# The first stage of a two-layer transformer tower: head sums turned by DVE and a DMA round trip, and the next batch's steps in other bursts

## The reference, cut to what matters

```
emb = x @ W + pe                                  # 1024 x 128, kept in H
n0  = layernorm(emb)                              # without gain and bias
Q, K, V = n0 @ Wq.T + bq, n0 @ Wk.T + bk, n0 @ Wv.T + bv
Q, K, V = (t.reshape(B * 8, 1024, 16) for t in (Q, K, V))   # a plain reshape: a "head" is 128 tokens x 8 pieces of 16 columns
context = softmax(Q @ K.T / 4) @ V                # reshaped back to 1024 x 128
r   = context @ Wo.T + bo + n0
H   = emb + layernorm(r) * gamma + beta           # the residual stream
mean1, rstd1 = moments of H; score1 = (layernorm of H) . attn_w   # for the next stage
```

## Time and profile before

| | us |
|---|---|
| median of 3 runs (1563.72 to 1567.42) | 1564.57 |
| the profiled execution | 1566.77 |
| its span in the trace | 1564.5 |
| first exponential of the first stage | 61.7 |
| the last copy of psO in the first stage | 669.5 |
| PE, DVE, ACT busy over the whole span | 1250.5, 989.6, 1012.1 |

### The profile page before, as it was taken

One profiled execution on the slowest core, in us unless ns is written; L12 is line 12 of the kernel. 1 busy time (PEld: TensorE's weight loads), 2 busy tenths in 40 slices (PEclk: granted clock), 3 DMA queues, 4 the chain that ended last, 5 costly groups with the idle time before them and its releaser, 6 DMA issues. The chain is left out here.

```text
span 1564.5 us, 30966 instructions
## 1 busy us (share of the span) xinstructions
PE 1250.5 (80%) x9689; PEld 826.3 (53%) x9689; DVE 989.6 (63%) x2772; ACT 1012.1 (65%) x1358; POOL 520.9 (33%) x456
## 2 busy tenths in 40 slices
PE   3599999999999999926999994888870699999930
PEld 2244444444444444414777773777760577777720
DVE  5256666666666664333777876788641589999932
ACT  0387778777778888902888883444410688888820
POOL 3212222222222221210000001278775066666654
PEclk9599999999999999967999996888855799999975
DMA  3542424242425252001111100011112455555519
GB/s 89 88 97 46 93 49 97 45 93 49 95 47 97 42 102 36 2 9 48 34 48 34 47 7 12 4 40 46 46 47 101 113 146 147 151 149 151 151 44 299
DMA packets 134465, 118.97 MB, mean 76 GB/s; under 512 B 30459, under 2 KB 112310, under 8 KB 134350
## 3 DMA queue, kind: packets, MB, share of 16 engines
q1 hardware_dynamic: 114798, 93.72, 26.5%
q0 software_dynamic: 9216, 16.94, 3.2%
q10 hardware_dynamic: 10336, 6.82, 2.2%
HBM read 76.61 MB, written 42.37 MB: 76 GB/s over the span
## 5 line engine op out<-in xcount | busy, mean ns | idle before, releaser
L343 ACT ACTIVATE a_probs<-a_psS 128x1024 f32<-128x1024 f32 x512 | 491.2, 1031 | 125.5 <-PE a_psS L426 98.4
L438 PE MATMUL a_psO<-a_probs,a_v 128*32 128x256 f32 x4096 | 282.5, 395 | 24.7 <-DVE a_o_sb L643 23.9
L807 ACT ACTIVATE f_g_hi<-f_psH,f_b_hid 128x512 fp32r<-128x512 f32 x288 | 200.6, 696 | 56.4 <-PE f_psH L71 49.6
L922 DVE TENSOR_TENSOR f_g_lo<-f_g,f_g_hi 128x512 fp32r<-128x512 f32 x288 | 197.7, 688 | 54.6 <-ACT f_g L809 52.5
L1744 POOL DMA_INDIRECT result<-f_out,f_idx x160 | 184.2, 1151 | 118.4 <-DVEq L1768 62.8
L426 PE MATMUL a_psS<-a_qs,a_ks 50*128 50x512 f32 x1024 | 193.8, 457 | 26.6 <-issue 12.4
L809 ACT ACTIVATE f_g<-f_psH,f_b_hid 128x512 f32<-128x512 f32 x288 | 199.8, 694 | 0.0
L438 PEld LDWEIGHTS a_psO<-a_probs,a_v 128*32 128x32 f32 x4096 | 108.7, 111 | 170.1 <-issue 89.2
L426 PEld LDWEIGHTS a_psS<-a_qs,a_ks 50*128 50x128 f32 x1024 | 79.2, 191 | 99.6 <-ACT a_probs L343 46.4
L69 PE MATMUL f_psH<-f_x_hi,f_w_lo 128*128 128x512 f32 x288 | 125.3, 435 | 2.9 <-DVE f_w_lo L64 2.6
L69 PE MATMUL f_psY<-f_g_hi,f_w_lo 128*128 128x512 f32 x288 | 117.1, 407 | 8.5 <-DVE f_w_lo L64 6.2
(11 more groups left out here) (296 smaller groups left out, 2152.7 us busy)
## 6 DMA issues: line engine op xcount, KB each, us to landing
f_raw<-W SPq DMA_DIRECT2D x80, 256.0 KB
a_qs<-qparts SPq DMA_DIRECT2D x96, 128.0 KB, 4.7
a_ks<-kparts SPq DMA_DIRECT2D x84, 128.0 KB, 4.7
f_rows<-queue SPq DMA_DIRECT2D x40, 260.0 KB, 2.7
qparts<-a_parts SPq DMA_DIRECT2D x16, 512.0 KB, 2.8
f_raw<-w SPq DMA_DIRECT2D x32, 256.0 KB, 2.6
kparts<-a_parts SPq DMA_DIRECT2D x14, 512.0 KB, 3.2
out_y<-result SPq DMA_DIRECT2D x8, 512.0 KB, 14.0
```

What stands on the lines that cost most here:

```text
L343: nc.scalar.activation(probs[u % NPR][:, :], psS[score_buffer(u)][:, :, :].rearrange("p a n -> p (a n)"), ACT.Exp).then_inc(exp_done, 1)
L438: last = nc.tensor.matmul(psO[32 * g:32 * g + 32, a * HALF:(a + 1) * HALF], v[par][:, 2 * hp + p, kt, :], probs[u % NPR][:, cols:cols + HA ...
L807: nc.scalar.activation(g_hi[i][:, n, :], psH[n][:, :], ACT.Gelu, bias=b_hid[i][:, n:n + 1])
L922: nc.vector.tensor_tensor(g_lo[i][:, n, :], g[:, n, :], g_hi[i][:, n, :].bitcast(F32), ALU.subtract).then_inc(lo_done, 1)
```

## The change

It does six things in the first stage; the two helper functions that the diff adds repeat ones that are there.

1. The turn, the turn back and their copies go. DVE transposes psO in 32 x 32 blocks into o_t (at r = 7, in place of the copy), `divide` works there and transposes back into o_n, SP's new `spread` writes o_n to DRAM in four DMAs, waits for them, and reads the context back as ctxT in one.
2. `project` moves from burst r = 3 of the next pair to burst r = 0 of the pair after it (LATE = 2), and in the burst ahead of the weighing. `add_input` and `divide` are at r = 0.
3. STEPS, UPPER, LOWER and APPLY have other bursts; the half 0 of a batch finishes its last three parts in the next batch; the rescue is at m = 22.
4. SP's queue of a batch: spread of the pair before, load of x, redistribute of q and k of chunk 0, spread, redistribute of q and k of chunk 1, spread, spread.
5. The stack loads are four DMAs for each part, of 32 and 16 rows for each head, in place of six; they have one semaphore for each buffer and chunk, and units 0 to 31 wait for chunk 0 only. The guard rows are sent by POOL.
6. The clear of v is one memset of columns 16 to 31 to 1.

```diff
-    PIECES = ((0, 0, 0), (0, 1, 16), (1, 0, 32))
+    HIGH = (0, 1)
...
-    STEPS = {0: ("E", 0), 4: ("E", 1), 6: ("T", 0), 8: ("q", 0), 12: ("k", 0), 14: ("T", 1), 16: ("q", 1), 20: ("k", 1),
-             22: ("N", 0), 24: ("N", 1), 28: ("v", 0), 30: ("v", 1)}
+    STEPS = {1: ("E", 0), 3: ("E", 1), 5: ("T", 0), 7: ("q", 0), 9: ("k", 0), 11: ("T", 1), 13: ("q", 1), 15: ("k", 1),
+             17: ("N", 0), 19: ("N", 1), 27: ("v", 0), 29: ("v", 1)}
-    TURN, BACK, PROJECT = 1, 2, 3
-    RESCUE = 26
+    LATE = 2
+    RESCUE = 22
-    UPPER = {3: "add_bias", 7: "normal", 10: "moments", 11: "second", 13: "score"}
-    LOWER = {21: "add_bias", 23: "normal", 26: "moments", 27: "second", 29: "score"}
-    APPLY = {1: 0, 5: 1}
+    UPPER = {2: ("moments", 0), 4: ("second", 0), 6: ("score", 0), 10: ("add_bias", 1), 12: ("normal", 1), 18: ("moments", 1), 23: ("second", 1),
+             25: ("score", 1)}
+    LOWER = {26: ("add_bias", 0), 28: ("normal", 0)}
+    APPLY = {2: 0, 8: 1}
...
+            both = dram[ch].rearrange("(j d) a p t -> p (d a) j t", d=DH)
+            high = dram[ch].rearrange("(j d) a p t -> p d a j t", d=DH)[:, :, HIGH[kind], :, :]
             for p in range(2):
-                for piece in PIECES:
-                    rows = slice(64 * p + piece[2], 64 * p + piece[2] + DH)
+                for row, src in ((0, both[p]), (2 * DH, high[p])):
+                    rows = slice(64 * p + row, 64 * p + row + src.shape[0])
+                    eng.dma_start((qs, ks)[kind][par][rows, :, ch * HALF:(ch + 1) * HALF].bitcast(F32), src).then_inc(stack_in[par][ch], 16)
...
+            def spread(pair):
+                sp.wait_ge(norm_done, pair + 1)
+                for p in range(2):
+                    for cc in range(2):
+                        row = 64 * p + 32 * cc
+                        sp.dma_start(dctx[pair % 2][64 * cc:64 * cc + 64, p, :].rearrange("(i d) t -> d i t", d=DH),
+                                     o_n[row:row + DH, :].rearrange("d (i t) -> d i t", t=P)).then_inc(ctx_out, 16)
+                sp.wait_ge(ctx_out, (pair + 1) * 4 * 16)
+                if pair:
+                    sp.wait_ge(op_done, pair)
+                sp.dma_start(ctxT[:, :, :], dctx[pair % 2]).then_inc(ctx_in, 16)
             def batch(b, par, prior, more):
+                if prior:
+                    spread(b * HP - 1)
+                if b + 2 < B:
+                    sp.wait_ge(emb_ps, (b + 1) * CPB)
+                    load_x(b + 2, par)
+                for q in range(CPB):
+                    if more:
+                        redistribute(sp, b + 1, 1 - par, 0, q)
+                        redistribute(sp, b + 1, 1 - par, 1, q)
+                    spread(b * HP + q)
+                spread(b * HP + 2)
...
+                    if more and m == RESCUE - 1:
+                        send_guard(pool, b + 1, 1 - par)
...
             def clear(par):
-                nc.gpsimd.memset(v[par][:, :, :, :], 0.0)
-                pool.drain()
-                nc.gpsimd.memset(v[par][:, :, :, DH:DH + 1], 1.0)
+                nc.gpsimd.memset(v[par][:, :, :, DH:], 1.0)
...
             for kind, ch in FIRST:
                 embed_step(kind, ch, 0)
+            send_guard(pool, 0, 0)
             pool.drain()
             clear(1)
...
+                if u % (UNITS // CPB) == 0:
+                    pe.wait_ge(stack_in[par][u // (UNITS // CPB)], (b // 2 + 1) * STACK)
                 if u == 0:
-                    pe.wait_ge(stack_in, (b + 1) * STACK)
-                    pe.wait_ge(guard_in, (b + 1) * GUARD)
+                    wait_guard(pe, b)
...
             def project(pair):
-                pe.wait_ge(ctxT_done, pair + 1)
+                pe.wait_ge(ctx_in, (pair + 1) * 16)
...
+                    q, r = divmod(m, BPP)
+                    pair = b * HP + (q - LATE)
+                    if r == 0 and pair >= 0:
+                        pe.wait_ge(psA_free, uses.next())
+                        project(pair)
                     for u in (2 * m, 2 * m + 1):
                         weigh(b, par, u)
...
-                nc.vector.tensor_copy(o_sb[:, :], psO[:, :]).then_inc(o_evac, 1)
+                nc.vector.transpose(o_t[:, :, :].rearrange("p k e -> p (k e)"), psO[:, :]).then_inc(o_evac, 1)
             def divide(pair):
+                dve.drain()
+                nc.vector.reciprocal(rden[:, :].unsqueeze(2), o_t[:, :, DH:DH + 1])
+                dve.drain()
+                nc.vector.tensor_tensor(o_t[:, :, 0:DH], o_t[:, :, 0:DH], rden[:, :].unsqueeze(2).broadcast_to([P, CH // 32, DH]), ALU.mult)
+                dve.drain()
+                if pair:
+                    dve.wait_ge(ctx_out, pair * 4 * 16)
+                nc.vector.transpose(o_n[:, :], o_t[:, :, :].rearrange("p k e -> p (k e)")).then_inc(norm_done, 1)
...
+                    if r == 0 and (q >= LATE or prior):
+                        add_input(b * HP + (q - LATE), par if q >= LATE else 1 - par, (q - LATE) % HP)
+                    if r == 0 and (q or prior):
+                        divide(b * HP + (q - 1))
...
+            for part, half_ in UPPER.values():
+                if (part, half_) == ("add_bias", 1):
+                    for pair in range(B * HP - LATE, B * HP):
+                        add_input(pair, (B - 1) % 2, pair % HP)
+                finish(part, B - 1, half_)
```

More of the change, by code:

```diff
@@ L105, in standardise, with moments @@
     return last
+def moments(nc, dve, src, stat, mv, veps, var_done, tiles=TPC):
+    for i in range(tiles):
+        nc.vector.bn_stats(stat[:, i, :], src(i))
+    dve.drain()
+    for i in range(tiles):
+        nc.vector.bn_aggr(mv[:, i, :], stat[:, i, :])
+    dve.drain()
+    nc.vector.tensor_scalar(veps[:, :], mv[:, :, 1], EPS, None, ALU.add).then_inc(var_done, 1)
+def standardise(nc, src, dst, mv, rs, tiles=TPC):
+    for i in range(tiles):
+        last = nc.vector.tensor_scalar(dst(i), src(i), mv[:, i, 0:1], rs[:, i:i + 1], ALU.subtract, ALU.mult)
+    return last
 def embed_and_attend(nc, H, ident, half, mean1, rstd1, score1, ins, B, S, D, NH):
@@ L264, in _ @@
             sp.wait_ge(cleared, 2)
-            for ch in range(CPB):
-                redistribute(sp, 0, 0, 0, ch)
-            send_guard(0, 0)
+            redistribute(sp, 0, 0, 0, 0)
+            redistribute(sp, 0, 0, 0, 1)
             sp.wait_ge(cleared, 4)
             rounds(batch)
+            spread(B * HP - 1)
         @block.gpsimd
@@ L333, in _ @@
             rounds(batch)
-            for part in UPPER.values():
-                finish(part, B - 1, 1)
+            for part, half_ in UPPER.values():
+                finish(part, B - 1, half_)
         @block.scalar
@@ L477, in batch @@
                         embed_step(*STEPS[m], b + 1, 1 - par, psA[:, :])
-                    if r in (TURN, BACK, PROJECT) and (q or prior):
-                        pe.wait_ge(psA_free, uses.next())
-                        {TURN: turn, BACK: turn_back, PROJECT: project}[r](pair)
             pe.sem_inc(pv_done, NPR)
@@ L494, in _ @@
             rounds(batch)
-            uses = Tally((B - 1) * PSA_BATCH - PSA_PAIR + PSA_PAIR * HP)
-            for step in (turn, turn_back, project):
+            uses = Tally((B - 1) * PSA_BATCH - LATE + HP)
+            for pair in range(B * HP - LATE, B * HP):
                 pe.wait_ge(psA_free, uses.next())
-                step(B * HP - 1)
+                project(pair)
         @block.vector
@@ L630, in guard @@
                 if b:
[L631 removed]
+                    wait_guard(dve, b - 1)
                 dve.wait_ge(unsafe_done, b + 1)
@@ L686, in batch @@
                     if prior and m in UPPER:
-                        finish(UPPER[m], b - 1, 1)
+                        part, half_ = UPPER[m]
+                        finish(part, b - 1, half_)
                     if m in LOWER:
-                        finish(LOWER[m], b, 0)
+                        part, half_ = LOWER[m]
+                        finish(part, b, half_)
                     if more and m == RESCUE - 1:
@@ L716, in _ @@
             divide(out)
-            evacuate(out)
-            add_input(out, (B - 1) % 2, HP - 1)
-            for part in UPPER.values():
-                finish(part, B - 1, 1)
+            for part, half_ in UPPER.values():
+                if (part, half_) == ("add_bias", 1):
+                    for pair in range(B * HP - LATE, B * HP):
+                        add_input(pair, (B - 1) % 2, pair % HP)
+                finish(part, B - 1, half_)
 def rank(nc, dve, out, more, same, p, lower):
```

99 lines of the change are left out of this document (34 added, 65 removed).

## The result

The changed kernel takes 1572.47 us (median of 20 runs, 1568.8 to 1581.06) against 1567.43 for the kernel before (20 runs): ratio 1.0041, 95% interval 1.0029 to 1.0054. It is slower by 0.4%, where 1543 was forecast; the time lies above the range too.

The account below looks back on a forecast made before the run. It took ACT to bound bursts without extra work and PE those with E, q, k or v steps; -8.8 - 5.0 - 13 - 1.2 + 6 = -22.0 took the profiled 1566.77 to 1545, the median to 1543; range 1508 to 1566.

Parts of the forecast that it names:

- The new wait on SP's queue: Pair 0's context round trip by DMA, wanted at m16: back at 40.7 into the batch, 2 us more lost.
- Pairs 1 to 3 have room: Later context round trips of a batch: pair 1's context back by 56, wanted at 60; pairs 2 and 3 unhindered.
- Rival B: Round trip decides at m16 and m24, small stores landing after the loaded queue: batch 82, total 1583; chance 0.14.
- DVE's chain: DVE's work in m1 to m15: last product not readable before 38.3 into the batch, holding PE some 3 us.
- rival D: The DVE transposes cost 1.4 and not 0.69, 2 us per batch: 1552; chance 0.18 together with C.
- Rival A: DVE and the round trip never end last, batches 69.3 by PE and ACT alone: 1506; chance 0.16.
- Batch 7: Last batch, without steps: 15.04 per pair instead of 15.35, 1.2 us less.
- The tail: After the last weigh: round trip and projection end add_input at 680.3, +6 us; half 0's parts fit into that wait.
- Batch 0: First batch, without finish parts: turns and idles saved, two projections added, 5.0 us less than 80.5.
- The start: First scores wait for chunk 0 only, Pool sends guard rows: first exponential near 53, 8.8 us less.
- rival C: The start doesn't move, Pool's queue being late in full DMA engines: 1552; chance 0.18 together with D.

Follow-up runs that it names:

- spread_first: Changed kernel with SP sending the contexts between q's and k's redistribution instead of behind both; ratio 0.9724 to the kernel before.
- no_trip: Changed kernel without the contexts' store and load, project reading o_n directly (contexts in the wrong order); ratio 0.9721 to the kernel before.
- start_only: Kernel before with only the semaphores by buffer and chunk and the guard rows sent by Pool; ratio 0.9903 to the kernel before.
- guard_sp: Changed kernel with contexts sent between q's and k's redistribution, and guard rows back on SP behind the stack loads; ratio 0.9728 to the kernel before.
- again_2: The changed kernel measured a third time, unaltered, on a third chip; ratio 1.0082 to the kernel before.
- again: The changed kernel measured once more, unaltered; ratio 1.0030 to the kernel before.
- before_again: The kernel before measured against itself as if it were a new one; ratio 0.9969.

## Why the prediction was wrong, point by point

**The step that failed: "The new wait on SP's queue."** It took the chain in the right order and priced one link of it, k's store, as if nothing were ahead of it. k's store went in at 2.6, from a store in the earlier trace rows that had no load ahead. In the kernel before, with k's step four bursts behind q's, k's stores took 3.2 (median); with k's step two bursts behind q's the store follows q's loads, and it took 5.2 here (median of all 5.9). That moved everything behind it by as much: contexts issued at 35.5 instead of 32.7, landed at 41.3 instead of 38.0, back at 43.6 instead of 40.7. The 4.7 behind the loads in the earlier trace rows was in the working, and used for the contexts (5.3 in all, 5.8 measured), but not for the store one line earlier. From the end of m16's scores at 39.0 that means 4.5 us of idle and not 2, and behind it a slow projection, weigh and scores: 0.5, 0.9 and 0.5 more, where 0.8 was put down for a whole batch. Against spread_first, pair 2 is 5.2 longer and pair 3 2.5: without what pair 3 loses a batch would have been near 77.

**"Pairs 1 to 3 have room"** failed with it. SP takes its work one after the other: q1 is split at 180.0, but SP stands at pair 0's contexts until 183.7, so q1's store, k1's and pair 1's contexts all move back, and the contexts again land behind loads. The changed kernel's SP once more:

```profile
194.95 1.76 SPq L241 DMA_DIRECT2D a_ks<-kparts  x4
196.76 1.85 SPq L281 DMA_DIRECT2D contexts<-a_o_n  x4
203.46 0.34 SPq L286 DMA_DIRECT2D a_ctxT<-contexts  x1
```

The room was counted from k1 "done near 42"; k's loads start here at 52.6 and the context is asked for at 61.1, while the projection had its turn at 61.6 and idled for 1.66.

**Rival B had the outcome**, at about two thirds of its price: the round trip decides at m16 and m24, 4.3 us per batch above the forecast where it said 6.6, and beyond the 3.6 from which it decides. spread_first and no_trip show it: they take the wait away in two ways and give the same 8 us per batch. Its reason was only in small part the one at work. It wanted the small stores to land 9 us after their last issue; the contexts' landed 3.9 after it (179.76 to 183.68), 1 more than forecast, and most of the delay lay one link earlier, in k's store. 0.14 was too little for its outcome.

**Right, within 1 us:** DVE's chain. k1's read runs from 180.77 to 181.52, so it ends 39.2 into the batch (forecast 38.3, of which 0.85 were this read). In no_trip the projection of m16 starts right behind that read, 39.2 into batch 1, where 38.7 was forecast. The two transposes take 715 and 711 ns (forecast 0.69), so rival D is out. Without the round trip the sum would have been 38.7 + 0.6 + 1.0 + 32.3 = 72.6 for a batch; 71.6 was measured. Rival A's 69.3 is not reached even there: pairs 0 and 1 stay at 18.8 and 19.3, the pairs with the steps. Batch 7 (-1.8 for -1.2) holds.

**The tail is right by luck**: +5.6 for +6, but what ends last there is DVE and not the round trip. The changed kernel's rows of DVE, SP and PE:

```profile
682.31 0.87 DVE L111 BATCH_NORM_STATS2 a_stat_f<-all_H 128x6 f32<-128x128 f32 x4
...
685.24 0.34 SPq L286 DMA_DIRECT2D a_ctxT<-contexts  x1
...
688.01 0.41 DVE L701 TENSOR_TENSOR a_res<-a_psA,a_n 128x256 f32<-128x256 f32 x1
...
688.48 1.23 PE L500 MATMUL a_psA<-a_w_raw,a_ctxT 128*128 128x128 f32 x4 [8.03 <-DVE a_res L701]
```

The last context's load takes 2.1 us and is in at about 687.3. But in the order of the program DVE first does moments, second and score of half 0 (682.31 to 688.10), and only then reads the projection of the pair before, for which the last one waits. The prediction let these parts "fit into that wait"; they outlast it. no_trip has the same 9.9 us without any trip.

**Batch 0** was wrong by the same wait: its count has no term for the round trip at all. But SP's queue is as full as in any batch; its pair 2 idles for 7.40, the longest of the 14 waits. In spread_first batch 0 takes 73.8: 6.7 less than before, where 5.0 was forecast.

**The start** gave 5.8 of 8.8. Pool issues the four guard rows in 2.30 (0.58 each, cheaper than the 1 us assumed), but they are in 7.0 us after the last issue and not 2.3: the full DMA engines of rival C, in part. The Trainium skill (DMA: Bandwidth & Descriptors, Issuing engines are not separate DMA queues) says that DMAs of all engines end up on the same 16 DMA engines and interleave there, and that a second issuing engine saves only issue time. This case agrees: 56.1 by SP and 55.7 by Pool with the same loads ahead, 51.4 with the loads behind. What the prediction gave as the sources of the gain, Pool's queue and the wait for chunk 0 alone, bring 2.5 in start_only, where both are in; guard_sp shows that, with four-piece loads, Pool's queue is not needed. The other 3.3 came with the four-piece loads, which the start's term left out, as start_only's and the changed kernel's rows above suggest; besides them only the shorter clear of v differs there, and no run takes the two apart.

**What stays open.** By the last add_input the first stage is longer by 16.0 us in the profiled execution and by 16.0 in again_2's (689.67); between again and before_again, on two chips of the other sort, by 11.2 (687.40 and 676.17). The totals by their ratios say 0.4, 0.8 and 0.3%, 5 to 13 us. In again the time behind the last add_input was 8 us shorter than in before_again, though nothing in them differs. Such shifts of single executions were not settled; the comparison of the medians carries the size of the loss, and the landmarks the cause. By these numbers the first stage's loss in a typical execution may be anything from 5 to 16 us.

## What to carry to other kernels

In these runs a small DMA's price was not its bytes but what was in the DMA engines when it was issued, from SP's queue or Pool's. So price every link of a chain of DMAs in the order in which it is issued, and ask of each what the link before has put there. When a computation is moved closer to its neighbour, its DMAs move as well, and a store that used to meet empty engines may meet the neighbour's loads. Send first what someone waits for soonest, then the bulk.

## What the runs showed of the hardware that was not expected

- A store of 512 KB took 2.9 us with nothing ahead and 5.2 (median 5.9) behind 768 KB of loads; four stores of 32 KB took 5.8 behind one set of loads, 8.9 behind two.
- A round trip through DRAM in the idle tail, the contexts of the last pair: issued at 682.25, its load at 685.24. So the four stores took 3.0 alone, against 5.8 under load.
- A DVE transpose of 128 x 512 fp32 took about as long as a copy of that size (0.69 us), from PSUM (715 ns) and from SBUF (711 ns).
- Stack loads in four pieces, two of them of 32 partitions, moved more at first than six pieces of 16. The first row is the DMA rate from 247.8 to 256 in the kernel before (loads issued from 250.5), the second from 176.1 to 183.7 in the changed one (loads from 176.1), each in 40 slices:

```profile
GB/s 0 0 0 0 240 380 480 420 380 480 180 0 0 0 0 0 0 35 85 250 215 155 275 230 165 130 110 150 120 130 135 135 135 125 130 135 130 120 150 105
```

```profile
GB/s 0 0 0 0 0 27 146 291 329 399 324 205 199 130 102 108 140 140 113 135 205 248 221 189 205 167 170 119 97 119 130 62 84 30 0 0 0 0 0 0
```

  Behind the peak (399 for 275) both fell to between 100 and 250 GB/s, and a piece of 256 KB landed in 4.2 us where one of 128 KB took 4.7. The Trainium skill's rule on the ports (SBUF — State Buffer, Door 1: The DMA port swizzle) would allow up to twice the rate for a DMA on 32 partitions in place of 16. This case agrees in part: nearly twice the bytes per DMA in the same time, but at the start, where SP's and ACT's loads overlap, 199 GB/s against start_only's 148.
